# Ten unread transposes taken out between the second attention's first score tiles, and ten behind the first expert's early products

## The chip, the cores and the metric

The kernel runs on one core of a Trainium2 chip. Its time is device microseconds for one execution. TensorE (PE in the profile) does the matmuls and the transposes, VectorE is DVE, ScalarE is ACT, GpSimd is POOL.

## The reference

Two layers work on x, two batches of 1024 tokens by 256 numbers, with a context of 77 tokens by 192. The stages are cross-attention with a latent, a feed-forward layer, a second cross-attention, and a mixture of eight experts that each choose 257 of 1024 tokens. Shortened:

```python
x = x + L0_xattn(ctx_768, _layernorm(x), mask)   # 4 heads, 1101 keys
x = x + L0_ffn(_layernorm(x))                    # 256 -> 1024 -> 256, gelu
# second attention: 8 heads of 64 over 77 context tokens
q, k, v = x @ Wq, context @ Wk, context @ Wv
attn = softmax(einsum('bhid,bhjd->bhij', q, k) * scale)
x = x + einsum('bhij,bhjd->bhid', attn, v) @ Wo + bo
# experts
scores = softmax(einsum('bsd,ed->bse', x, router_w))
gate, sel = top_k(swapaxes(scores, 1, 2), 257)
h = gelu(einsum('becd,edh->bech', x[b_idx, sel], w1) + b1)
y = einsum('bech,ehd->becd', h, w2) + b2
x = x + zeros_like(x).at[b_idx, sel].add(y * gate)
```

## The kernel before

Each engine has one program, written out by hand, and semaphores order them against each other. What stands in TensorE's queue runs in the order in which the code issues it: a wait holds up all that is behind it.

The second attention goes over 16 tiles of 128 tokens (n = 0 to 15), in four groups of four (attention1(g)). For each tile scores(n) makes the scores of all eight heads in banks 4 and 5 of PSUM (12 matmuls of 128x308 in line 481, three passes with split operands). It can't start before VectorE has subtracted the maximum of the tile before out of the same banks: VectorE's scores(n) takes the maximum (line 1617, tile sm) and then writes the difference to Pb (line 1621), and that releases the banks. ScalarE makes the exponentials, GpSimd scales them, TensorE turns them (line 880) and product(n) multiplies them with the values. Before attention1(0) comes values_out, which makes the values (lines 807 to 827) while the feed-forward layer's last products run.

Between the attention and the experts the routing finds each expert's tokens. index(ex) makes the positions of expert ex (8 small matmuls for each batch, line 1076) once VectorE has made oh (line 1888); GpSimd then gathers the tokens' rows to gt; gathered(ex) transposes them (line 1096), ScalarE and VectorE split them to the two GT tiles (lines 1973 and 1909). first_product(ex, m, c) is a part of the first expert layer: block m of 128 hidden numbers, half c of the tokens (0: 256 columns, 1: 258 columns), 6 matmuls. For expert 0 the three products of half 0 (m = 0 to 2) run early, before the second half of the rows is turned. The loop over experts then runs over all the others, with index(1) between.

At eleven places in TensorE's code (fourteen in its queue, 238 transposes in all) warm(m, n) issues n transposes of the identity into bank m, line 475. Nothing reads their result:

```python
def warm(m, n):
    clear(m)
    for _ in range(n):
        pe.transpose(bank[m][:, 0:128], ident[:, :], ident[:, :])
```

Of the kernel before, what the change touches and what calls it, by code (L numbers as in the profile page):

```python
# [95 lines left out]
def build(nc, A, out, y_dram):  # L96
    with ExitStack() as root:
# [359 lines left out]
        def tensor_program(pe):  # L457
# [8 lines left out]
            def clear(b):  # L466
                if busy[b]:
                    pe.wait_ge(*busy[b])
                    busy[b] = None
# [6 lines that stand above are left out]
# [360 lines left out]
            def scores(n):  # L836
                g, t = n // 4, n % 4
                b, c = g // 2, 512 * (g % 2) + 128 * t
                clear(4)
                clear(5)  # L840
                if t == 0:
                    pe.wait_ge(v_xt, 2 * (8 + g) + 2)
                if n == 0:
                    pe.wait_ge(v_wk, 8)
                for u in range(2):
                    w_ = slice(308 * u, 308 * u + 308)
                    op = three(bank[4 + u][:, 0:308], [((xt[0][:, k, c:c + 128], xt[1][:, k, c:c + 128]),
                                                        (WK[0][:, b, k, w_], WK[1][:, b, k, w_])) for k in range(2)])
                op.then_inc(p_s, 1)
                busy[4] = busy[5] = (v_sub, n + 1)  # L850

            def product(n):
                b, T, m = n // 8, PT1[n % 2], 1 + n % 2
                K = [128, 128, 128, 128, 104]
                clear(m)
                pe.wait_ge(v_pT, n + 1)
                if n == 0:
                    pe.wait_ge(v_vw, 6)
                three(bank[m][:, 0:256], [((T[0][0:K[c], c, :], T[1][0:K[c], c, :]),
                                           (VW[0][0:K[c], b, c, :], VW[1][0:K[c], b, c, :])) for c in range(5)]).then_inc(p_pv, 1)  # L860
                busy[m] = (v_x1, n + 1)

            def attention1(g):
                if g == 0:
                    scores(0)
                    warm(1, 10)
                    scores(1)
                    yield
                    yield
                for t in range(4):  # L870
                    n = 4 * g + t
                    if n + 2 < NT:
                        scores(n + 2)
                    yield
                    clear(6)
                    clear(7)
                    pe.wait_ge(g_pb, n + 1)
                    o = ps[:, 6:8, :].rearrange("p u n -> p (u n)")
                    for c in range(5):
                        op = pe.transpose(o[:, 128 * c:128 * c + 128], Pb[n % 3][:, 128 * c:128 * c + 128], ident[:, :])  # L880
                    op.then_inc(p_pT, 1)
                    busy[6] = busy[7] = (v_pT, n + 1)
                    yield
                    if n:
                        product(n - 1)
                        yield
                    yield
                if g == 3:
                    product(NT - 1)
# [124 lines left out]
            drain(sd, vw_)  # L1014
            sd = queries(1, q_)
            merge(attention1(0), (sd, 0.6))
            drain(sd)
            for g in range(1, 3):
                qs = queries(g + 1, q_)
                rs_ = both(idle(6 if g == 1 else 3), route_norm(g - 1), idle(3 if g == 1 else 6), route_pick(g - 1, (0,), 0, 0))  # L1020
                merge(attention1(g), (qs, 0.6), (rs_, 1.0))
                drain(qs, rs_)
            rs_ = both(idle(3), route_norm(2), idle(8), route_pick(2, (0, 3), 0, 3))
            merge(attention1(3), (rs_, 1.0), (both(idle(12), route_norm(3)), 1.0))
            last_routes(rs_, route_norm(4), route_pick(3, (4,), 7, 4), route_pick(4, (5,), 6, 5))

# [39 lines left out]
            def index(ex, lead=7, apart=3):  # L1066

                yield from idle(lead)
                for b in range(B):
                    if b:  # L1070
                        yield from idle(apart)
                    if b == 0:
                        clear(2)
                    pe.wait_ge(v_oh, 2 * ex + b + 1)
                    for t in range(8):
                        op = pe.matmul(bank[2][:, 15 * b:15 * b + 15], oh[b][:, t, :],
                                       bv[ex % 2][:, 8 * b + t, :, :].rearrange("p s v -> p (s v)"), start=t == 0, stop=t == 7)
                    op.then_inc(p_ix, 1)
                    yield
                busy[2] = (v_idx, ex + 1)  # L1080
                yield
# [55 lines left out]
                first_product(0, m, 0)  # L1137
            next(rows)
            next(rows)
            warm(1, 10)  # L1140
            second = index(1, 4, 0)
            for _ in range(4):
                next(second)
# [1746 lines left out]

        sync_program(nc.sync)
        tensor_program(nc.tensor)
        vector_program(nc.vector)
        scalar_program(nc.scalar)
# [56 lines left out]
```

## Time and profile before

| | us |
|---|---|
| median of 3 runs | 821.63 |
| lowest, highest | 821.62, 821.73 |
| the profiled execution | 820.28 |
| its span (first to last instruction) | 818.2 |
| mean granted TensorE clock | 0.978 |
| TensorE busy in the span | 758.7 (93%) |
| VectorE busy in the span | 529.2 (65%) |

Times in the profile are microseconds from the start of the span. A granted clock of 1.00 is 2.4 GHz, one of 0.50 is 1.2 GHz. The profiled execution is one of its own, 1.35 us shorter than the median of the timed runs.

### The profile page before, as it was taken

The page shows a single profiled execution, that of the slowest core. Times are in us where ns is not written, and L with a number is a line of the kernel's source. Part 1 is how long each engine was busy: PE and PEld are TensorE (multiplying, and loading weights), DVE is VectorE, ACT ScalarE, POOL GpSimd, SP SyncE. Part 2 cuts the span into 40 slices and gives each one's busy share as a digit, 9 for nine tenths or more (in the row PEclk, how much of TensorE's full clock was granted, in tenths as well). Part 3 has the DMA queues.
Part 4 walks back from the last instruction along what each step waited for, and adds up shares of the span by engine and source line. Part 5 has one row for each costly group of instructions (what it writes and reads, how often), then busy time and mean ns, then how long its engine had stood idle before and what let it go on. Part 6 is the DMA issues. An engine that isn't in the chain of part 4 may idle for free.

```text
span 818.2 us, 12847 instructions
## 1 busy us (share of the span) xinstructions
PE 758.7 (93%) x4881; PEld 620.0 (76%) x4881; DVE 529.2 (65%) x1163; ACT 399.3 (49%) x699; POOL 322.0 (39%) x281
## 2 busy tenths in 40 slices
PE   8889999999999999999999989994689999999995
PEld 8655556656755564679889888883689999999995
DVE  7767875773677683357455498885747655667552
ACT  3655643573466344563472245433035765557650
POOL 6502002100201022066361143334336878888793
PEclk9999999999999999999999999996799999999998
DMA  7000000000000100100030201111212545544432
GB/s 186 2 1 1 1 1 1 1 1 1 1 1 1 52 4 0 52 1 3 1 98 2 103 2 52 53 65 52 104 29 83 144 109 151 145 99 127 126 33 32
DMA packets 21509, 39.31 MB, mean 48 GB/s; under 512 B 4913, under 2 KB 16905, under 8 KB 19145
## 3 DMA queue, kind: packets, MB, share of 16 engines
q1 hardware_dynamic: 14793, 30.07, 11.1%
q0 software_dynamic: 6656, 8.43, 5.9%
q8 instruction: 39, 0.64, 0.3%
q14 instruction: 21, 0.17, 0.1%
HBM read 29.96 MB, written 8.40 MB: 47 GB/s over the span
## 4 chain that ended last, share of the span: by engine, by line
PE 56%; DVE 14%; ACT 4%; issue 3%; POOL 3%; DVEq 0%; ACTq 0%
PE ps L481 18%; PE ps L650 8%; PE ps L1173 6%; PE ps L1176 5%; PE ps L754 5%; PE ps L671 2%; PE ps L672 2%; PE ps L612 2%; PE ps L475 1%; DVE rep L1811 1%; DVE sm L1617 1%; PE ps L1096 1%; DVE Pb L1621 1%; POOL out_dram L2733 1%; DVE sm L1626 1%
## 5 line engine op out<-in xcount | busy, mean ns | idle before, releaser
L650 PE MATMUL ps<-PT,VA 128*65 128x512 f32 (+1 forms) x288 | 147.9, 595 | 3.6 <-ACT PT L2120 3.3
L2120 ACT ACTIVATE PT<-ps 128x512 f32<-128x512 f32 x128 | 76.1, 595 | 71.0 <-PE ps L672 70.8
L481 PE MATMUL ps<-GT,wh 128*128 128x258 f32 (+1 forms) x768 | 94.7, 284 | 0.4 <-DVE GT L1909 0.4
L481 PEld LDWEIGHTS ps<-GT,wh 128*128 128x128 f32 x768 | 92.7, 189 | 0.6 <-DVE GT L1909 0.6
L2733 POOL DMA_INDIRECT out_dram<-ye,idx x40 | 69.7, 1743 | 19.8 <-issue 10.9
L2417 ACT ACTIVATE het<-ps,b1e 128x514 f32<-128x514 f32 x64 | 44.3, 692 | 58.4 <-PE ps L481 54.0
L1944 DVE TENSOR_TENSOR he<-het,he 128x514 fp32r<-128x514 f32 x64 | 46.4, 726 | 35.6 <-ACT he L1973 35.1
L671 PE MATMUL ps<-QA,KA 128*128 128x512 f32 x144 | 67.7, 470 | 0.8 <-ACT QB L1973 0.8
L2467 POOL TENSOR_TENSOR rs<-rs,half 128x4 f32<-128x4 f32 (+2 forms) x19 | 18.2, 958 | 119.7 <-DVE rs L1214 91.3
L2477 POOL TENSOR_TENSOR ssq<-ssq,half 128x8 f32<-128x8 f32 x12 | 19.7, 1638 | 108.3 <-DVE ssq L1295 108.3
L2611 POOL DMA_INDIRECT gt<-y_dram,idx x40 | 46.4, 1159 | 40.2 <-DVE gate L1899 30.4
L612 PE MATMUL ps<-KA,QA 128*128 128x368 f32 x192 | 59.1, 413 | 3.0 <-ACT mrt L1973 0.8
L612 PEld LDWEIGHTS ps<-KA,QA 128*128 128x128 f32 x192 | 33.4, 188 | 36.9 <-DVE x L1423 15.6
L650 PEld LDWEIGHTS ps<-PT,VA 128*65 128x65 f32 (+1 forms) x288 | 38.5, 138 | 29.2 <-ACT PT L2120 9.8
L1409 DVE TENSOR_REDUCE mxp<-ps 128x1 f32<-128x736 f32 x64 | 58.5, 914 | 0.2 <-PE ps L612 0.2
L1407 DVE TENSOR_REDUCE mxp<-ps 128x1 f32<-128x368 f32 x64 | 34.5, 539 | 36.5 <-PE ps L612 35.6
L672 PE MATMUL ps<-QB,KB 65*128 65x512 f32 x144 | 57.1, 397 | 0.0
L1173 PE MATMUL ps<-he,wh 128*128 128x258 f32 x384 | 54.8, 291 | 0.6 <-DVE he L1944 0.6
L481 PE MATMUL ps<-wo,OT 65*128 65x258 f32 x192 | 53.3, 386 | 0.2 <-DVE x L1423 0.2
L481 PEld LDWEIGHTS ps<-wo,OT 65*128 65x128 f32 x192 | 31.2, 189 | 27.8 <-issue 24.5
L754 PE MATMUL ps<-w2e,hT 128*128 128x256 f32 x384 | 50.5, 286 | 0.0
L1176 PE MATMUL ps<-wh,he 128*128 128x256 f32 x384 | 50.2, 284 | 0.0
(291 smaller groups left out, 1662.8 us busy)
## 6 DMA issues: line engine op xcount, KB each, us to landing
wr<-in_w1e_dram SPq DMA_DIRECT2D x8, 1024.0 KB, 5.1
wr<-in_w2e_dram SPq DMA_DIRECT2D x8, 1024.0 KB, 4.9
x<-in_x_dram SPq DMA_DIRECT2D x4, 512.0 KB, 6.7
w<-in_w_dram SPq DMA_DIRECT2D x2, 1024.0 KB, 4.7
y_dram<-yr SPq DMA_DIRECT2D x3, 512.0 KB, 3.0
out_dram<-x SPq DMA_DIRECT2D x3, 512.0 KB, 4.1
b2r<-in_b2r_dram SPq DMA_DIRECT2D x8, 128.0 KB, 3.1
gt<-y_dram,idx POOLq DMA_INDIRECT x40, 3.0
```

Of the source, the lines that this page charges most:

```text
L481: op = pe.matmul(o, l, r, start=n == 0, stop=n == len(calls) - 1)
L612: op = pe.matmul(ps[:, j, 0:368], QA[:, h, 128 * qt:128 * qt + 128], KA[:, h, 368 * j:368 * j + 368], start=True, stop=True)
L650: pe.matmul(bank[6 + hf][0:65, :], VA[b][0:K, kt, h, :], PT[u % 4][0:K, :], start=kt == 0, stop=kt == 8).then_inc(p_pv, 1)
L671: pe.matmul(bank[m][0:K, :], KA[:, h, ks], QA[:, h, qc], start=True, stop=False)
L672: pe.matmul(bank[m][0:K, :], KB[:, h, ks], QB[:, h, qc], start=False, stop=True).then_inc(p_s, 1)
L754: op = pe.matmul(bank[bk][:, 0:256], l, r, start=n == 0, stop=n == 23)
L1173: op = pe.matmul(bank[dc][:, 0:258], w2h[i][:, wc_], he[j][:, m, 256:514], start=n == 0, stop=n == 23)
L1176: op = pe.matmul(bank[dc][:, 0:256], he[j][:, m, c0:c0 + 128], w2h[i][:, 256 * m:256 * m + 256], start=n == 0, stop=n == 23)
L1409: v.tensor_reduce(mxp[:, qt, 0:1], ps[:, 0:2, 0:368], AX.XY, ALU.max).then_inc(v_mx, 1)
L1944: v.tensor_tensor(he[1][:, m, :], het[m % 2][:, :], f(he[0][:, m, :]), ALU.subtract).then_inc(v_he, 1)
L2120: a.activation(PT[u % 4][0:K, :], bank[4 + u % 2][0:K, :], ACT.Exp, bias=0.0 if K == 128 else mcol[:, b:b + 1]).then_inc(a_exp, 1)
L2733: g_.indirect_dma_start(out, bass.IndirectOffsetOnAxis(ap=idx[0:M, ex, s_:s_ + 1], axis=0), ye[ex % 2][0:M, s_, :], None, compute_op=ALU.a ...
```

## The change

Two calls of warm are taken out of TensorE's program, ten transposes each. The other nine calls, with 218 transposes, stay. No other engine's program is touched, and no wait is taken out but that for bank 1 inside warm.

```diff
             def attention1(g):
                 if g == 0:
                     scores(0)
-                    warm(1, 10)
                     scores(1)
                     yield
                     yield
...
                 first_product(0, m, 0)
             next(rows)
             next(rows)
-            warm(1, 10)
             second = index(1, 4, 0)
             for _ in range(4):
                 next(second)
```

The first place in TensorE's queue, as the difference of the two orders (WK holds the keys' side of the scores, xt the turned tokens; the two rows ahead are the end of scores(0), those behind the start of scores(1)):

```order
 L481 MATMUL ps<-WK_142,xt_50 128x308 x2
 L481 MATMUL ps<-WK_141,xt_50 128x308 x2
-L475 MATMUL ps<-ident 128x128 x10
 L481 MATMUL ps<-WK_141,xt_51 128x308 x2
 L481 MATMUL ps<-WK_142,xt_50 128x308 x2
```

Only the ten transposes are gone; scores(1) now stands directly behind scores(0).

The second place in TensorE's queue before, from the transposes of the last gathered rows (line 1096) over half 1 of product m = 0 to the index product of expert 1:

```order
L1096 MATMUL ps<-ident,gt_191 128x128 x2
L1096 MATMUL ps<-ident,gt_191 128x2
L475 MATMUL ps<-ident 128x128 x10
L481 MATMUL ps<-GT_193,wh_186 128x258 x2
L481 MATMUL ps<-GT_194,wh_185 128x258 x2
L481 MATMUL ps<-GT_193,wh_185 128x258 x2
L1076 MATMUL ps<-bv_182,oh_179 128x15 x8
```

And the same place after the change, where lines below the edits have moved up by one:

```order
L1095 MATMUL ps<-ident,gt_191 128x128 x2
L1095 MATMUL ps<-ident,gt_191 128x2
L481 MATMUL ps<-GT_193,wh_186 128x258 x2
L481 MATMUL ps<-GT_194,wh_185 128x258 x2
L481 MATMUL ps<-GT_193,wh_185 128x258 x2
L1075 MATMUL ps<-bv_182,oh_179 128x15 x8
```

Again only the ten transposes are gone, and the product follows the gathered rows directly.

## Rows read from the trace of the kernel before

**Rows 1.** The page, part 2: the granted clock in tenths, 40 slices of the span.

```profile
PEclk9999999999999999999999999996799999999998
```

**Rows 2.** Timeline, all engines, first place: start us, us, engine, line, operation, [idle before <-releaser].

```profile
463.86 2.06 PE L481 MATMUL ps<-WK,xt 128*128 128x308 f32 x12
...
465.76 1.25 PE L475 MATMUL ps<-ident 128*128 128x128 f32 x10
...
465.96 0.80 DVE L1617 TENSOR_REDUCE sm<-ps 128x8 f32<-128x616 f32 x1
...
466.79 0.80 DVE L1621 TENSOR_TENSOR Pb<-ps,sm 128x616 f32<-128x616 f32 x1
...
467.74 1.94 PE L481 MATMUL ps<-WK,xt 128*128 128x308 f32 x12 [0.72 <-DVE Pb L1621]
...
469.71 0.80 DVE L1617 TENSOR_REDUCE sm<-ps 128x8 f32<-128x616 f32 x1 [2.12 <-PE ps L481]
```

**Rows 3.** The chain that ended last, in order of time: start us, us, what.

```profile
466.79 0.81 DVE Pb L1621
467.74 1.96 PE ps L481 x12
...
609.44 7.97 PE ps L481 x66
```

**Rows 4.** Timeline, all engines, second place.

```profile
604.50 1.05 PE L1096 MATMUL ps<-ident,gt 128*128 128x128 f32 x6
...
605.49 1.31 PE L475 MATMUL ps<-ident 128*128 128x128 f32 x10
605.49 0.94 DVE L1909 TENSOR_TENSOR GT<-ps,GT 128x258 fp32r<-128x258 f32 x2 [3.26 <-ACT GT L1973]
...
606.55 0.97 PE L481 MATMUL ps<-GT,wh 128*128 128x258 f32 x6
606.67 2.35 DVE L1888 TENSOR_TENSOR oh<-slots,place 128x1024 bf16<-128x1024 bf16 x2
...
608.03 0.35 PE L1076 MATMUL ps<-bv,oh 128*128 128x15 bf16 x8 [0.51 <-DVE oh L1888]
```

**Rows 5.** Windows: length, busy us (count) of PE, PEld, DVE, ACT, POOL; granted clock; DMA.

```profile
34.50:42.50 8.00, 6.16 (x36) 4.58 (x35) 5.71 (x11) 2.07 (x5) 5.27 (x4) 1.00 0.01 2
471.50:475.00 3.50, 3.10 (x21) 2.63 (x21) 3.40 (x7) 3.50 (x7) 2.64 (x3) 1.00 0.00 0
609.30:813.00 203.70, 200.69 (x1726) 196.78 (x1722) 125.19 (x208) 117.06 (x196) 154.01 (x103) 1.00 0.41 104
...
147.72:151.13 3.41, 3.41 (x15) 2.50 (x13) 0.43 (x1) 1.55 (x3) 0.29 (x1) 0.50 0.00 0
...
543.70:547.05 3.35, 3.35 (x18) 3.35 (x17) 2.26 (x5) 0.97 (x2) 1.22 (x1) 0.50 0.64 216
...
576.90:581.20 4.30, 4.30 (x22) 4.24 (x22) 3.12 (x9) 0.00 (x0) 2.56 (x2) 0.50 0.46 191
581.25:583.80 2.55, 1.96 (x18) 1.71 (x17) 2.13 (x9) 0.00 (x0) 1.27 (x1) 1.00 0.00 0
```

**Rows 6.** Timeline of TensorE alone at five other places.

```profile
147.10 2.44 PE L481 MATMUL ps<-wqk,xt 128*128 128x256 f32 x12 [0.88 <-DVE OT L1429]
...
471.49 1.93 PE L481 MATMUL ps<-WK,xt 128*128 128x308 f32 x12 [1.38 <-DVE Pb L1621]
...
543.38 1.04 PE L880 MATMUL ps<-ident,Pb 128*128 128x128 f32 x5 [1.92 <-DVE PTx L1653]
544.08 3.36 PE L481 MATMUL ps<-VW,PTx 128*128 128x256 f32 x15
...
547.75 2.03 PE L481 MATMUL ps<-VW,PTx 128*128 128x256 f32 x15
...
576.83 2.80 PE L475 MATMUL ps<-ident 128*128 128x128 f32 x12
...
579.50 2.34 PE L475 MATMUL ps<-ident 128*128 128x128 f32 x12
```

## The prediction

> **What bounds the kernel now.** I read the page first. Its row of granted clock is full nearly everywhere, with a dip in two slices next to each other and one at the very end [rows 1]; in a slice of 20 us a fall of 3 us still reads as 9. A kernel that keeps TensorE this busy can lose time through that clock, so I then looked at the two places of the change in the timeline, all engines together.
>
> At the first place the reader is to see who is waited for. scores(0) runs on TensorE from 463.86 for 2.06 us, so to 465.92. VectorE takes its maximum at 465.96 and its subtraction ends at 466.79 + 0.80 = 467.59; scores(1) starts at 467.74, since both score tiles use banks 4 and 5. The ten transposes lie between, at 465.76 for 1.25 us, and TensorE is still idle for 0.72 us behind them [rows 2]. So here VectorE sets the pace, and the chain that ended last goes through the subtraction and then scores(1), not through the transposes [rows 3].
>
> At the second place the transposes start at 605.49 and take 1.31 us. The product behind them needs the last GT tile, which VectorE finishes at 605.49 + 0.94 = 606.43; the product starts at 606.55. Then the index product waits for oh until 608.03, 0.51 us idle [rows 4]. From 609.44 the chain is TensorE alone [rows 3], and to the end of the experts it is busy for 200.69 of 203.70 us at full clock [rows 5]: whatever TensorE loses there is lost in full.
>
> **What the edit removes, at a constant clock.** Twice ten transposes, nothing else: no wait, no DMA and no other engine's work. First place: scores(1) is released by VectorE at 467.59, with or without them: gain 0. Its upper bound would be the whole 1.25 us if the transposes held it back, which the 0.72 us of idle time behind them excludes. Second place: the product could start as soon as GT is there, 606.43 and the usual tenth of a microsecond, so 606.5: at most 0.1 us earlier. And that is not passed on, because the next index product still waits for oh, whose two operations start on VectorE at 606.67, right behind its own work, and which nothing on TensorE releases: gain 0, bounds 0 and 0.1. The bank wait inside the first call (bank 1) is met by that time, and the first product(0) asks for it again later. At a constant clock the change is worth nothing.
>
> **What the edit does to the clock.** The removed work filled idle time. After the change TensorE rests from 465.92 to 467.74, 1.8 us in one piece, and at the second place from 605.5 to 606.5, works for 0.97 us, and rests again for 0.51 us [rows 2, 4].
> What such rests do is in the trace. At 543.38 TensorE resumed after 1.92 us of rest, and from 543.7 the granted clock was 0.50, that is 1.2 instead of 2.4 GHz, to 547.1 [rows 5, 6]. At 147.10 it resumed after only 0.88 us of rest, and from 147.7 to 151.1 the clock was again 0.50 [rows 5, 6]. Against that, 1.38 us of rest before 471.49 brought no fall: the clock is 1.00 over the next 3.5 us [rows 5, 6]. Nor did the stretch from 34.5 to 42.5, where TensorE rests for 8.00 - 6.16 = 1.84 us in several pieces [rows 5]. So 1.8 us in one piece is nearly the case that fell, and 1.0 + 0.5 us with work between is between the two kinds. Neither is certain.
>
> The Trainium skill has a rule that speaks against any effect: TensorE: Matmul & The Clock Gate, Part 4: PE-mode transpose, says that transposes in transpose mode do not count as TensorE activity for the clock, so that they don't bring it to full. By that rule the twenty transposes held nothing up, and taking them out costs 0. The trace disagrees where it can be read: 24 such transposes (line 475) from 576.83 and 579.50 on are nearly all that TensorE does until 581.2, at clock 0.50, and from 581.25 the clock is 1.00 [rows 5, 6]. So the clock rose behind transposes alone, and I go by the rows.
>
> **The price of one fall.** Two groups of 15 matmuls of the same shape (128x256): 3.36 us at the low clock (544.08), 2.03 us at the full one (547.75) [rows 6]. That is 1.66 times as long, or 1.33 us lost in a fall of 3.4 us when TensorE is what all wait for.
> First place: falls came 0.3 us (543.7) and 0.6 us (147.7) after the engine resumed. So one would begin at 468.0 to 468.4, with 1.3 to 1.7 us of scores(1) still to run (it ends at 469.68); 0.66 times that is 0.9 to 1.1 us, and VectorE's next maximum, at 469.71, waits for it [rows 2]. The later part of the fall lies in the 1.38 us rest before 471.49 and is free. The bounds: 0.2 us if it begins at 469.3 (only the end of scores(1) is slow), 1.3 us if all 1.94 us of it is slow. I take 0.8.
> Second place: it would begin between 606.9 and 608.6. What is slow before 609.2 is partly hidden by the wait for oh; the rest is the dense stretch of products. Of 3.4 us some 0.1 to 1.0 us is hidden: 1.33 less 0 to 0.4. Bounds 0.4 (the fall begins at once and mostly passes in the waits) and 1.35. I take 1.3.
> What follows a fall: all later work comes later against the clock, and with it the stretches that are already near a fall. The one at 543.7 may go (up to -1.3 us, were all of it on the path; about half, since POOL's Pb is waited for soon after) or another may come before it (up to +1.3 us). I count 0, and give the range its width by it.
>
> **The sum.** No fall: 0. One fall: +0.8 or +1.3, middle +1.05. Both: +2.1. Against the profiled execution, which took 820.28 us (818.2 of span and 2.1 around it), that is 821.3 or 822.4 us. The median of the runs is 821.63, 1.35 us above the profiled one, about the price of one fall, so their clock need not have been the same; I add the change to the median.
>
> **The rivals.**
> A (forecast, 0.40): the clock falls at one of the two places, or at each in only part of the executions. +0.8 to +1.3, so 822.7 us. For it: one fall after less rest than here, none after similar rests, so that more than the length of a rest decides it.
> B (0.30), the other side of no change: the clock falls at both places in every timed run. +2.1 us, 823.7 us, 0.26% slower. For it: the 1.92 us rest that fell is like the 1.8 us here, and the fall after 0.88 us makes the second place possible. It decides when both falls come in the same execution and neither is given back later: from +1.64 us on it is measurable.
> C (0.23): no fall at either place. 821.6 us. For it: the rests before 471.49 and between 34.5 and 42.5.
> D (0.07): the transposes do hold up the path, which the timeline cannot show if the wait behind them is passed late. Then up to 1.0 us comes back at the second place (606.5 to 605.5) and up to 1.25 at the first: 819.4 us, 0.27% faster. Against it: 0.72 us of idle time behind the first ten, and VectorE's 606.43.
>
> **How the numbers follow.** A measurement of this kernel tells a change from none at about 0.2%, which is 1.64 us: 820.0 to 823.3. A lies in that but for a tenth of it (0.36 of 0.40), C all of it (0.23), of B a tenth, where something is given back (0.03): same 0.62. Slower: 0.27 of B and 0.04 of A, 0.31. Faster: D, 0.07. The predicted time is A's, 822.7 us, with a range of its own of 822.2 to 823.2. The range for all: down to 820.9, so C with 0.7 us given back at 543.7, and up to 824.3, so B with 0.6 us more; outside lie D and the far ends of B.
>
> **What the changed profile would show.** Right at a constant clock: scores(1) still starts about 1.8 us behind the end of scores(0), now with that as idle time put down to VectorE's Pb; the index product still starts about 1.6 us behind the last GT tile. Right on the clock: a stretch of granted clock 0.50 of some 3.4 us that begins just behind scores(1) or in the first expert's first products, with 12 matmuls of scores taking about 3 us instead of 1.94, or the 66 products up to 1.3 us more than 8.12. It would be wrong if both stretches stay at 1.00 and the time still moves by over 0.5 us, if the falls of before (147.7, 543.7) move and account for more than the new ones, or if the start of scores(1) or of the index product comes earlier by over 0.2 us against what precedes it.

## The result and the profile after

| | before | after |
|---|---|---|
| median, us | 821.59 (20 runs) | 823.78 (20 runs) |
| lowest to highest, us | 820.41 to 823.08 | 821.08 to 827.39 |
| profiled execution, us | 820.28 | 825.21 |
| its span, us | 818.2 | 823.1 |
| its mean granted clock | 0.978 | 0.971 |

The ratio is 1.0029 with a 95% interval of 1.0017 to 1.0040: slower by 2.2 to 2.4 us. The spread has grown as well, from 2.7 to 6.3 us. Of the twenty executions after, the seven with a mean granted clock of 0.979 or more have a median of 822.10 us; the ten at 0.974 or less took 824.37 to 827.39 us.

The profiled execution after is at the long end. The page has its clock in the same 40 slices as [rows 1]:

```profile
PEclk9999999999999999999999899995699999999998
```

There is an 8 in slice 23 of the 40, where before had a 9, and the dip in slices 28 and 29 is deeper. The first place in the timeline of all engines (lines below the first edit have moved up by one or two), to be read beside [rows 2]:

```profile
462.58 2.06 PE L481 MATMUL ps<-WK,xt 128*128 128x308 f32 x12
...
465.51 0.80 DVE L1619 TENSOR_TENSOR Pb<-ps,sm 128x616 f32<-128x616 f32 x1
...
466.45 2.66 PE L481 MATMUL ps<-WK,xt 128*128 128x308 f32 x12 [1.82 <-DVE Pb L1619]
...
469.15 0.80 DVE L1615 TENSOR_REDUCE sm<-ps 128x8 f32<-128x616 f32 x1 [2.85 <-PE ps L481]
...
470.93 3.41 PE L481 MATMUL ps<-WK,xt 128*128 128x308 f32 x12 [0.96 <-DVE Pb L1619]
...
474.38 0.80 DVE L1615 TENSOR_REDUCE sm<-ps 128x8 f32<-128x616 f32 x1 [1.20 <-PE ps L481]
```

scores(1) starts 3.87 us behind scores(0), against 3.88 before: nothing is gained. It then takes 2.66 us instead of 1.94, and scores(2) takes 3.41 us instead of 1.93. VectorE waits for both: 2.85 us for scores(1), where it was 2.12 before, and 1.20 us for scores(2), where it did not wait before. The second place in TensorE's timeline, beside [rows 4]:

```profile
607.33 1.05 PE L1095 MATMUL ps<-ident,gt 128*128 128x128 f32 x6
609.32 0.98 PE L481 MATMUL ps<-GT,wh 128*128 128x258 f32 x6 [0.94 <-DVE GT L1907]
610.86 0.36 PE L1075 MATMUL ps<-bv,oh 128*128 128x15 bf16 x8 [0.57 <-DVE oh L1886]
611.08 1.64 PE L481 MATMUL ps<-GT,wh 128*128 128x258 f32 x6
612.52 0.43 PE L1075 MATMUL ps<-bv,oh 128*128 128x15 bf16 x8
...
612.80 8.72 PE L481 MATMUL ps<-GT,wh 128*128 128x258 f32 x66
621.36 0.89 PE L1171 MATMUL ps<-he,wh 128*128 128x258 f32 x6
```

The index product starts 3.53 us behind the gathered rows, as before (608.03 - 604.50 = 3.53). The six products behind it take 1.64 us instead of 0.96, the 66 take 8.72 instead of 8.12. The rows of the kernel before that these and the next comparisons go by:

```profile
473.66 0.79 DVE L1617 TENSOR_REDUCE sm<-ps 128x8 f32<-128x616 f32 x1
...
556.36 2.67 PE L920 MATMUL ps<-rw,xf 128*128 128x8 f32 x16
...
608.23 0.96 PE L481 MATMUL ps<-GT,wh 128*128 128x258 f32 x6
...
609.29 8.12 PE L481 MATMUL ps<-GT,wh 128*128 128x258 f32 x66
617.25 0.89 PE L1173 MATMUL ps<-he,wh 128*128 128x258 f32 x6
```

The windows of the kernel after (length, busy us and count of PE, PEld, DVE, ACT, POOL, then the granted clock) say why both places are slow:

```profile
466.45:467.35 0.90, 0.90 (x6) 0.90 (x7) 0.00 (x0) 0.61 (x1) 0.00 (x0) 1.00 0.00 0
467.37:474.19 6.82, 5.86 (x25) 5.42 (x24) 3.92 (x7) 3.17 (x6) 2.39 (x3) 0.50 0.00 0
474.20:477.60 3.40, 2.56 (x20) 2.36 (x19) 2.65 (x4) 1.91 (x3) 0.89 (x4) 1.00 0.02 5
...
610.73:614.14 3.41, 3.28 (x28) 3.21 (x29) 1.73 (x2) 2.25 (x4) 0.00 (x0) 0.50 0.00 0
...
590.25:597.07 6.82, 5.71 (x36) 5.63 (x33) 5.53 (x16) 0.00 (x0) 0.00 (x0) 0.50 0.00 0
```

The clock falls behind both rests, at 467.4 for 6.8 us and at 610.7 for 3.4 us. The last row is a third fall, at 590.2, where nothing was edited; whether it follows from the change is not shown. The falls at 147.7 and 543.7 of [rows 5] are missing from this execution. The first of them lies ahead of both edits, so its absence is not the change's. At the second, the rest of 1.92 us before Pb's transposes is the same, and the 15 matmuls behind it now run at full speed:

```profile
544.14 0.74 PE L879 MATMUL ps<-ident,Pb 128*128 128x128 f32 x5 [1.92 <-DVE PTx L1651]
544.63 2.03 PE L481 MATMUL ps<-VW,PTx 128*128 128x256 f32 x15
```

So one and the same rest is followed by a fall in one execution and not in another. Read against the shift of a landmark, the 4.9 us between the two spans come in pieces. A landmark is a row that both timelines have; how much more its time has shifted than that of the landmark ahead of it is what was lost between the two. The subtraction of tile 0 ends 1.28 us earlier than before (the fall at 147.7 is missing). The maximum of tile 2, at 474.38 us, is 0.72 us later than the 473.66 of before, so the first place took 2.0 us. The gathered rows at the second place are 2.83 us later (607.33 for 604.50). The 2.1 us between are a balance: 0.5 are won by the missing fall at 543.7; 0.9 are lost by the last routing group, whose 16 products take 3.46 us for 2.67 because the low clock reaches them earlier; 0.5 in the flag rounds, where the low clock lasts longer; and 1.2 in the fall at 590.2. The second layer of expert 0 starts 4.11 us later (621.36 for 617.25), so the second place took 1.28 us. The last 0.8 us arise just behind, at a wait for GT of expert 1. That wait turns out below not to belong to the change.

### The profile page after: what moved, and what is told of

Read it like the earlier page. It is cut to its first block, busy times and chain, and to the rows that moved or that the text cites. A ratio compares the mean times of both kernels' runs of the same rounds, so it can differ in the third digit from the quotient of the medians.

```text
span 823.1 us, 12807 instructions
## 1 busy us (share of the span) xinstructions
PE 761.3 (92%) x4861; PEld 622.2 (76%) x4861; DVE 526.7 (64%) x1163; ACT 399.1 (48%) x699; POOL 323.2 (39%) x281
## 4 chain that ended last, share of the span: by engine, by line
PE 57%; DVE 13%; ACT 4%; issue 4%; POOL 3%; DVEq 0%; ACTq 0%
PE ps L481 19%; PE ps L650 8%; PE ps L1171 6%; PE ps L1174 5%; PE ps L754 5%; PE ps L671 2%; PE ps L672 2%; PE ps L612 2%; PE ps L475 1%; DVE sm L1615 1%; DVE rep L1809 1%; PE ps L1095 1%; DVE Pb L1619 1%; POOL out_dram L2731 1%; ACT htmp L2179 1%
```

## The experiments

| kernel | executions | median us | ratio to before, 95% interval | mean granted clock |
|---|---|---|---|---|
| first place alone | 12 | 823.69 | 1.0017 (1.0005 to 1.0029) | 0.9759 |
| second place alone | 12 | 822.88 | 1.0011 (0.9996 to 1.0026) | 0.9772 |
| ordinary matmuls instead | 12 | 822.39 | 1.0001 (0.9989 to 1.0014) | 0.9787 |
| two more rests filled | 12 | 820.00 | 0.9975 (0.9962 to 0.9988) | 0.9841 |
| before, beside these four | 35 | 822.18 | | 0.9791 |
| the changed kernel again | 12 | 824.33 | 1.0035 (1.0016 to 1.0055) | 0.9750 |
| and the flag rounds filled too | 11 | 819.04 | 0.9966 (0.9954 to 0.9977) | 0.9885 |
| changed, two other rests filled | 12 | 822.37 | 1.0003 (0.9989 to 1.0018) | 0.9794 |
| five transposes for ten | 12 | 822.53 | 1.0010 (0.9997 to 1.0022) | 0.9784 |
| before, beside these four | 34 | 821.83 | | 0.9794 |

The mean granted clock is the mean over a kernel's executions of the value that each has over its span. Each ratio is to the executions of before that ran beside it.

**First place alone.**

```diff
                     scores(0)
-                    warm(1, 10)
                     scores(1)
```

> Only the ten transposes between the first two score tiles are taken out; those behind the early products stay. Clock theory (the whole effect comes from falls of the granted clock at the two places, in those executions where the rest falls badly): the median is 0.5 to 1.5 us above the kernel before, about half of the whole change's 2.2 us, with executions in two groups: some like before (about 821.5 us), some 2 us longer. In the profile, either no clock of 0.50 between 464 and 476 us, and scores(1) takes 1.94 us, or a fall there with scores(1) or scores(2) at 2.5 to 3.4 us. Rival (the second place alone costs, since only from there on TensorE is the bound): within 0.3 us of before.

0.17% slower, 1.4 us, with an interval from 0.4 to 2.4 us, so the rival's 0.3 us is out. The two groups of executions that had been expected did not come: they are spread from 821.92 to 825.25 us. The profiled one is the shortest, and its clock did not fall here.

```profile
462.20 2.06 PE L481 MATMUL ps<-WK,xt 128*128 128x308 f32 x12
466.07 1.94 PE L481 MATMUL ps<-WK,xt 128*128 128x308 f32 x12 [1.82 <-DVE Pb L1620]
469.83 1.94 PE L481 MATMUL ps<-WK,xt 128*128 128x308 f32 x12 [1.38 <-DVE Pb L1620]
```

From scores(0) to scores(2) it takes 469.83 - 462.20 = 7.63 us, and in [rows 2, 6] 471.49 - 463.86 = 7.63 us. At a constant clock the ten transposes are worth nothing, to 0.01 us. This execution has a fall of 6.8 us from 587.2 on, though, which the profile of before has not.

**Second place alone.**

```diff
             next(rows)
-            warm(1, 10)
             second = index(1, 4, 0)
```

> Only the ten transposes behind the early products are taken out; those between the score tiles stay. Clock theory: 0.5 to 1.5 us above before, in two groups of executions, about 821.5 and about 823.5 us; the profile shows either no fall between 603 and 616 us or one that makes the 66 products behind the second index product longer than 8.1 us. Rival (the first place alone costs, since a fall there also reaches scores(2)): within 0.3 us of before.

0.11% slower, with an interval that just reaches zero; the two parts together are 0.28%, beside 0.29% and 0.35% measured for both. By the time alone the rival, less than 0.3 us, is not excluded. But the profiled execution has the fall, and the 66 products take 9.29 us instead of 8.12:

```profile
602.88 1.05 PE L1096 MATMUL ps<-ident,gt 128*128 128x128 f32 x6
604.86 0.99 PE L481 MATMUL ps<-GT,wh 128*128 128x258 f32 x6 [0.94 <-DVE GT L1908]
606.41 0.35 PE L1076 MATMUL ps<-bv,oh 128*128 128x15 bf16 x8 [0.56 <-DVE oh L1887]
606.61 1.22 PE L481 MATMUL ps<-GT,wh 128*128 128x258 f32 x6
607.63 0.42 PE L1076 MATMUL ps<-bv,oh 128*128 128x15 bf16 x8
607.91 9.29 PE L481 MATMUL ps<-GT,wh 128*128 128x258 f32 x66
617.04 0.89 PE L1172 MATMUL ps<-he,wh 128*128 128x258 f32 x6
```

From the gathered rows to the second layer: 14.16 us, against 12.75 before. Up to there the fall costs 1.41 us.

**Ordinary matmuls instead.**

```diff
+            def plain(m, n):
+                clear(m)
+                for _ in range(n):
+                    pe.matmul(bank[m][:, 0:128], ident[:, :], ident[:, :], start=True, stop=True)
...
-                    warm(1, 10)
+                    plain(1, 5)
...
-            warm(1, 10)
+            plain(1, 5)
```

> At both places five ordinary matmuls of the identity with itself, 128x128, stand in for the ten transposes; each leaves two records of 109 ns, so TensorE is busy as long as before. What is computed for the output is unchanged. Clock theory: any work of the same length keeps the clock as transposes do, so 821.6 us, within 0.5 us of before, and no fall at the two places. Rival (transposes don't count as activity, so that ordinary matmuls hold the clock better than they do): faster than before by 0.5 us or more. Second rival (it is the order of the instructions that counts, not the clock): also like before, so this run tells only the first rival apart.

1.0001, and no fall at either place in the profile. No difference between ordinary matmuls and transposes can be told. The interval reaches from 0.9 us faster to 1.2 us slower, so the first rival's "0.5 us or more" is cut down to 0.5 to 0.9 us, not excluded. If transposes did nothing for the clock, this kernel would be faster than before by all that the change costs, 2.2 us, and that is outside. This bears on the rule of the Trainium skill that the prediction weighed (TensorE: Matmul & The Clock Gate, Part 4: PE-mode transpose), by which transposes don't count for the clock. The measurement disagrees with it: taking the transposes out costs 0.29%, and ten of them do as well as five ordinary matmuls within the interval.

**Two more rests filled.** The kernel before, with transposes added:

```diff
+                    if n == 14:
+                        warm(2, 10)
                     clear(6)
                     clear(7)
                     pe.wait_ge(g_pb, n + 1)
...
+                if r == 4:
+                    warm(5, 9)
                 pe.wait_ge(a_z, 4 + r + 1)
```

> The kernel before with transposes added where TensorE rests at two more places: ten into bank 2 ahead of tile 14's transposes of Pb (the rest of 1.92 us before 543.38), and nine into bank 5 ahead of the last routing group's rows (the rest of 1.04 us before 555.66). Clock theory: the fall at 543.7 no longer comes in any execution and that at 557.3 comes later; 0.6 to 1.5 us faster than before, and fewer long executions. Rival (transposes added on an engine that is 93% busy only delay what is behind them): 0 to 2 us slower.

0.25% faster, 2.0 to 2.2 us, more than expected. The profile shows the two rests filled and the work behind them fast (the 16 small products of the last routing group were 2.67 us before and 3.46 us after):

```profile
539.61 1.26 PE L475 MATMUL ps<-ident 128*128 128x128 f32 x10
541.68 0.74 PE L882 MATMUL ps<-ident,Pb 128*128 128x128 f32 x5 [0.82 <-DVE PTx L1657]
542.17 2.03 PE L481 MATMUL ps<-VW,PTx 128*128 128x256 f32 x15
...
552.25 1.15 PE L475 MATMUL ps<-ident 128*128 128x128 f32 x9
553.46 0.66 PE L908 MATMUL ps<-ident,yr 128*128 128x128 f32 x4
554.16 1.92 PE L924 MATMUL ps<-rw,xf 128*128 128x8 f32 x16
```

**The changed kernel again.** No edit.

> The changed kernel once more, unchanged, beside the kernel before on the same chip. Clock theory: the sum of the two parts measured alone (0.17% and 0.11%), so 0.2 to 0.4% slower, with a mean granted clock about 0.005 under that of before. Rival (the parts overlap, since one fall shifts the other place out of reach): under 0.17%.

1.0035. The profiled execution has a fall at the first place alone, and a short one of 3.4 us:

```profile
462.60 2.06 PE L481 MATMUL ps<-WK,xt 128*128 128x308 f32 x12
...
466.47 2.92 PE L481 MATMUL ps<-WK,xt 128*128 128x308 f32 x12 [1.82 <-DVE Pb L1619]
...
471.21 1.94 PE L481 MATMUL ps<-WK,xt 128*128 128x308 f32 x12 [0.96 <-DVE Pb L1619]
```

scores(1) takes 2.92 us, scores(2) takes 1.94 again, and scores(2) starts 8.61 us behind scores(0) instead of 7.63: this fall costs 0.98 us. Its second place, without a fall, takes 3.53 us from the gathered rows (604.23) to the index product (607.76), as in [rows 4], and 12.76 us to the second layer (616.99), where before took 12.75.

**The flag rounds filled too.** On top of the two rests:

```diff
                 if n >= 6:
                     warm(1, 12)
+                elif n >= 1:
+                    warm(1, 7)
                 pe.wait_ge(v_sel, n + 1)
```

> The version with transposes added at two more places, and besides seven transposes in each of five earlier rounds of the flag search (rounds 1 to 5, where TensorE rests 1.77 us of each 1.95 us and the clock is 0.50); at the low clock seven take about 1.5 us and fit into the rest. Clock theory: the clock rises before round 6, so that the first two groups of twelve take 1.3 instead of 2.8 and 2.3 us; 0.5 to 1.0 us faster than that version, so 0.3 to 0.4% faster than before. Rival (each group delays its flag product, as the groups of twelve do by 0.2 us even at the full clock): no gain, or up to 1 us slower than that version.

0.34% faster than before, the fastest version here, and the one with the least spread (818.04 to 819.68 us). The step from the version before it is 0.9 of a thousandth across two sets of runs, not a comparison of its own. The profile shows how the rounds keep their pace of 1.95 us while the clock rises at 570.3, four us before the groups of twelve:

```profile
568.31 0.18 PE L1042 MATMUL ps<-flag,same 128*128 128x1 bf16 x1 [0.17 <-DVE flag L1820]
568.36 1.73 PE L475 MATMUL ps<-ident 128*128 128x128 f32 x7
570.26 0.18 PE L1042 MATMUL ps<-flag,same 128*128 128x1 bf16 x1 [0.17 <-DVE flag L1820]
570.31 0.96 PE L475 MATMUL ps<-ident 128*128 128x128 f32 x7
...
574.20 1.51 PE L475 MATMUL ps<-ident 128*128 128x128 f32 x12
```

The first group of twelve takes 1.51 us, where it took 2.80 [rows 6].

**Changed, two other rests filled.** The changed kernel with warm(2, 10) and warm(5, 9) as above.

> The changed kernel with the nineteen transposes added at the two other places: twenty out, nineteen in. Clock theory: the effects add, +0.28% and -0.25%, so within 0.15% of the kernel before; the mean granted clock within 0.002 of it. Rival (the number of transposes counts, so that the same number gives the same time whatever the place): also the same, so this tells it apart only from a theory in which the two places of the change matter by their waits: then 0.25% faster than before, as the added ones alone.

1.0003: within the interval the effects add. The mean clock is that of before, 0.9794. This run cannot separate the clock from the mere number of transposes, as had been said ahead of it. The other runs speak against the number: 20 taken out cost 0.29 to 0.35%, 19 added give 0.25%, but 35 more give only 0.09%. The profiled execution has both new falls and none behind the rest filled at 543 us; at the first place again a long one, with scores(2) at 3.42 us, and at the second the 66 products take 9.45 us.

```profile
466.25 2.18 PE L481 MATMUL ps<-WK,xt 128*128 128x308 f32 x12 [1.82 <-DVE Pb L1623]
470.25 3.42 PE L481 MATMUL ps<-WK,xt 128*128 128x308 f32 x12 [0.96 <-DVE Pb L1623]
...
608.12 9.45 PE L481 MATMUL ps<-GT,wh 128*128 128x258 f32 x66
```

**Five transposes for ten.**

```diff
-                    warm(1, 10)
+                    warm(1, 5)
...
-            warm(1, 10)
+            warm(1, 5)
```

> Five transposes in place of ten at each of the two places, so half of each rest is filled. Clock theory: falls get rarer faster than in proportion, as the two rests are then 1.3 us and 0.4 us long; within 0.1% of before, and no fall at either place in the profile. Rival (a cost in proportion to what is left out, whatever its mechanism): half of the whole change, 0.14% slower.

1.0010 with an interval from 0.9997 to 1.0022 holds both theories: inconclusive. The profiled execution has rests of 1.27 and 0.24 us and no fall at either place.

## Why the prediction was right, and what in it was not

The time, 823.78 us, lies in the range of 820.9 to 824.3, and the two mechanisms that the forecast and rival B share, no gain at a constant clock and a loss through falls behind the two rests, were right. The likeliest case was not: of the chances most (0.62) lay on no difference that can be told, and the measured 0.29% is rival B's size.

- **Worth nothing at a constant clock:** shown at the first place by the run without its transposes and without a fall (7.63 and 7.63 us), at the second by the changed kernel's second profile (3.53 and 3.53 us to the index product, 12.76 and 12.75 us to the second layer). Rival D is out.
- **The clock falls behind the rests:** shown. With the first place's transposes gone, three of four profiles have a fall there (two of the changed kernel, one of the swapped, none of the first place alone); at the second place three of four too (two of the three of the changed and the swapped kernel, and the second place alone). Of the six profiles that have filler at the first place, and the six that have it at the second, none has a fall there. Rival C is out.
- **The price of one fall at the first place:** 0.8 was taken, with bounds of 0.2 and 1.3, and this is the term that was mis-sized. A short fall (the changed kernel again) costs 0.98 us. The two long ones cost 2.0 us (changed kernel) and 1.5 us (swapped; scores(3) starts 13.11 us behind scores(0), against 11.57 before), both above the bound. The step that failed reads: "The later part of the fall lies in the 1.38 us rest before 471.49 and is free." In the two long cases the fall lasted 6.8 us instead of 3.4 and so reached scores(2), which took 3.4 instead of 1.93 us. The falls of 3.4 us in the trace of before were taken for the only length. It also began later in these two, 0.9 and 1.5 us behind the start of scores(1), where 0.3 to 0.6 was taken; 0.6 us held for the short one.
- **The price of one fall at the second place:** 1.3 was taken, with 1.35 as the bound; up to the second layer 1.28, 1.41 and 1.42 us were measured (the last from 603.24 and 617.41 us in the swapped kernel). What failed is "whatever TensorE loses there is lost in full". A little further on TensorE waits for GT of expert 1, and that wait takes up a part. From the gathered rows to the end of the span, the six profiles without a fall there, other than the one of before, take 215.5 to 215.7 us; the three with one take 215.8, 216.1 and 217.0. So 0.1 to 1.3 us of a fall is left at the end.
- **One fall or two:** case A was a single fall, or falls in part of the executions, priced as if half of them had none. Falls do come in part of the executions, but in more than half: 3 in 4 at either place, as far as four profiles tell. So B's time came about by A's mixture: not both falls in every execution, but frequent ones, and larger ones at the first place. By the prices at the places themselves, 1.0 to 2.0 and 1.3 to 1.4 us, that gives 0.75 x 1.5 + 0.75 x 1.35 = 2.1 us on average. That this equals B's +2.1 is partly luck, since the second price shrinks by the end and other falls come and go.
- **What follows a fall:** counted as 0 with a spread of 1.3 us. Here the profiles show a pattern that is too small a sample to settle. Where the rest before 543 was not filled, all five profiles without a fall at the first place have a fall behind it, and both with one have none (the changed kernel, twice). And a fall of 6.8 us that begins at 587 or 590 us came in two profiles only, both of kernels without the first ten transposes, once with a fall at the first place and once without. So from scores(0) to the gathered rows the cost differs from that at the place itself: it is 140.6 to 140.7 us in the four profiles that have filler there and at neither other rest, and 1.0, 1.3 and 4.1 us more in the three without it (the changed kernel again, the first place alone, the changed kernel); the swapped kernel takes 2.4 us more than the one with the two other rests filled. The mean of these four is 2.2 us, that at the second place 0.5 (0 where there is no fall). The first place is the dearer one, as in the times of the two parts (1.4 and 0.9 us). Whether the later falls follow from the change stays open.

The wait for GT of expert 1 is not the change's. Before's profile does not have it; the other nine do, with 0.3 to 1.4 us, among them the two kernels that keep the transposes at both places. The same transposes in the profile of before, and then with two more rests filled:

```profile
619.88 0.53 PE L1096 MATMUL ps<-ident,gt 128*128 128x128 f32 x3
```

```profile
617.61 0.59 PE L1100 MATMUL ps<-ident,gt 128*128 128x128 f32 x3 [1.38 <-DVE GT L1913]
```

From the gathered rows to these transposes it is 15.4 us in the profile of before and 16.9 in each of the six others without a fall there; to the end of the span it is 213.7 us, and at least 215.5 in every other. So of the 4.9 us between the two profiled spans, 2.1 lie behind the gathered rows and next to nothing of them is the change's: before's profiled execution was a short one. With the two rests filled, ScalarE begins its part of GT at 615.92, 1.75 us behind the transposes that it needs (614.17); in the profile of before it is 0.42 us. Why is open.

Over all kernels, time goes by and large with the clock. An execution with mean clock c spends 2 x (1 - c) of its span at 0.50, since the profiles show only 0.50 and 1.00: 34.3 us for before (0.9791), 39.6 for the first place alone, 41.1 for the changed kernel again (0.9750, beside 33.8), 26.0 with two rests filled and 18.8 with the flag rounds too. The mean times beside them differ from those of before by +1.6, +2.6, -2.2 and -2.8 us. The time that the edits add at the low clock costs 0.3 to 0.4 us for each us of it (1.6 over 5.3, 2.6 over 7.3), near the 0.4 worked out from the two groups of 15 matmuls. In the flag rounds, where TensorE mostly waits, a low clock costs less: there some 7 us fewer of it gave 0.6 us.

Open is why a fall lasts 3.4 us in one execution and 6.8 in another, the exact share of executions with a fall, and how much of the price is in falls elsewhere.

## What to carry to other kernels

Work whose result nobody reads can be worth its place: take the idle time that remains without it from the trace, and look whether the granted clock falls behind rests of that size anywhere in the program. Price a fall by rows at both clocks and let it reach the next group of matmuls too; and take several profiles, since one execution shows only one draw. Here rests of 1 to 2 us ahead of work that others wait for were the ones to fill, with a filler that ends before the wait does; filled at two more rests and in five short rounds, they gave 0.34%. And compare with more than one profile of the kernel before: the one here lacked a wait that all the others had, and was about 2 us shorter behind it.

## What the runs showed of the hardware that was not expected

A rest of 1.92 us ahead of the same five transposes was followed by a clock of 0.50 in one execution and by 1.00 in another of nearly the same program. Falls at one place, behind a rest of 1.82 us, lasted 3.4 or 6.8 us. The clock rose from 0.50 to 1.00 at 570.3 us in rounds of 1.95 us with seven transposes and one small matmul each. The median of three executions (821.63, within 0.11 us) had looked like a kernel with hardly any spread; twenty executions spread over 2.7 us.
